# Reordering a load queue: a block's rows and first bias ahead of its second-layer weights in the mixed rounds of an expert stage

## The chip, the cores and the metric

One Trainium2 chip, one core, one program. The metric is the device time of one execution in microseconds (us); the time of a kernel is the median of its runs. The hardware profiler took one execution of the kernel before, and every row below comes from that execution. Its engines are TensorE (PE; PEld is its weight load), VectorE (DVE), ScalarE (ACT), GpSimd (POOL) and the queue of SyncE (SP), which issues nearly all loads.

## The reference

A one-layer vision transformer over 16 images of 256 tokens, width 256: patch embedding, gated decay attention, and a mixture of experts. The change lies in the last part, which computes

```python
logits = xf @ w_router
probs = jax.nn.softmax(logits, axis=-1)
topk_w, topk_idx = jax.lax.top_k(probs, TOP_K)
mask = jax.nn.one_hot(topk_idx, NUM_EXPERTS, dtype=xf.dtype)
weights = jnp.sum(topk_w[..., None] * mask, axis=1)
h = jnp.einsum('te,ieh->tih', xf, w1) + b1
h = jax.nn.gelu(h)
out = jnp.einsum('tih,ihe->tie', h, w2) + b2
out = jnp.sum(out * weights[..., None], axis=1)
```

with 4096 tokens, 8 experts, two experts to a token, width 256 and hidden width 1024, all in float32.

## The kernel before, in words

The engines run five hand-written instruction streams that meet through counting semaphores; no scheduler reorders them. Each stream is in order: an instruction that waits holds up all behind it on its engine.

The expert stage gathers the tokens of one expert into blocks. 31 blocks of 256 rows and 9 units of 128 rows are worked through in a fixed order, numbered by j. j = 0 to 21 are blocks (a first kind up to 3, then plain ones). From j = 22 on, blocks and units alternate: 9 rounds of one block and one unit, called the **mixed rounds**. A block splits its weights, rows and activations into a high and a low part and multiplies three times (L1494, L1506). A unit multiplies once in float32 straight from the loaded weights (L1519, L1530).

A block or unit j needs five loads: its rows from `expert_rows` (261 KB for a block, L402; half for a unit, L408), weights of layer 1 and 2 (1024 KB each, L388 and L392), the bias of layer 1 (4 KB, L396) and the bias of layer 2, spread to all partitions (128 KB, L399).

In one mixed round, call the block m, its unit u, and the next block n. TensorE's order is fixed: second half of layer 1 of m; transpose of u's rows (L1276); first half of layer 2 of m; first half of layer 1 of u (L1519); second half of layer 2 of m (L1506); transpose of n's rows (L1276, it waits for them to land); second half of layer 1 of u; half of layer 2 of u (L1530); first half of layer 1 of n; the rest of layer 2 of u.

The second half of layer 1 of u writes over four PSUM banks, so its first matmul waits until ScalarE has done the gelu of u's first chunk. That gelu (L887, into `q_s` or `k_s`; of the eight chunks of a block it goes into `mid_f`) waits for both biases of u on one semaphore:

```python
if c == 0:
    act.wait_ge(M[f"b_in{k.par}"], 32 * (k.n + 1))
```

The loads are issued by `load_pair(one, nxt, after, parity)`, once per round, eight times in all; there `one` is u, `nxt` is n and `after` is the block behind n. Its steps and the waits in them:

- `load_one(u)`: rows of u, w1 and b1 of u, then w2 of u when the unit before has finished its layer 2 (L570).
- `weights2_ahead(n)`: w2 of n, when VectorE has converted w2 of m (L556).
- `bias2(u)`: b2 of u, when the output of the unit before is taken (`y_done`).
- `rows_whole(n)`: rows of n, when VectorE has worked out the weights of m's rows (L531, `wsel_done`, set by L1918; m's rows lie in the same buffer), then b1 of n when ScalarE has done all gelus of m (L533, `gel_done`).
- `weights1_ahead(after)`: w1 of the block behind n (L550).
- `bias2(n)`: b2 of n, when m's output is taken (L1925).

Between the steps SP reads the expert's number and the list's place from a table (L411, L414). ScalarE converts w2 of n (L881) between the gelus of u, from the fifth on; VectorE follows with the low part (L1932). All these loads go through SP's one DMA queue; GpSimd issues the scattered additions to the output (L711).

Of the kernel before, what the change touches and what calls it, by code (L numbers as in the profile page):

```python
# [75 lines left out]
def vit_layer(nc, xT, w_tok, gamma, wq, wk, wv, wg, wa, ba, wo, gn_w, gn_b,  # L76
# [3 lines left out]
    with ExitStack() as ctx:  # L80
# [266 lines left out]
        def _(sp):  # L347
# [39 lines left out]
            def load_w1(e, staged, m):  # L387
                sp.dma_start(staged.rearrange("p (k n) -> p k n", k=EC),  # L388
                             w1[bass.ds(e, 1), :, :].rearrange("a (k p) n -> (a p) k n", p=P)).then_inc(M[m], 16)

            def load_w2(e, staged, m):
                sp.dma_start(staged.rearrange("p (k n) -> p k n", k=HC),  # L392
                             w2[bass.ds(e, 1), :, :].rearrange("a (k p) n -> (a p) k n", p=P)).then_inc(M[m], 16)

            def load_b1(e, par):
                sp.dma_start(b1_sb[par], b1[bass.ds(e, 1), :, :].rearrange("a p k -> (a p) k")).then_inc(M[f"b_in{par}"], 16)  # L396
# [4 lines left out]
            def load_rows(r, par):  # L401
                sp.dma_start(rows_f[par], lists_d[bass.ds(r, BLK), :].rearrange("(s p) n -> p s n", p=P)).then_inc(M[f"row_in{par}"], 16)  # L402
# [4 lines left out]
            def load_unit(r, par):  # L407
                sp.dma_start(rows_f[par][:, 0, :], lists_d[bass.ds(r, P), :]).then_inc(M[f"row_in{par}"], 16)  # L408

            def expert(j):  # L410
                return sp.value_load(tab[0:1, bass.ds(j, 1)], min_val=0, max_val=X - 1)  # L411

            def place(j):
                return sp.value_load(tab[0:1, bass.ds(j + NT, 1)], min_val=0, max_val=X * CAP)  # L414
# [110 lines left out]
            def rows_whole(k):  # L525

                e, r = expert(k.j), place(k.j)
                if isinstance(k.b, int) and k.b < 2:
                    sp.wait_ge(M["o_ps"], 2 * NP * NPR)
                sp.wait_ge(M["xe_ps"], EC * (k.j - 1))  # L530
                sp.wait_ge(M["wsel_done"], k.j - 1)  # L531
                load_rows(r, k.par)
                sp.wait_ge(M["gel_done"], HC * (k.j - 1))  # L533
                load_b1(e, k.par)

            def bias2(k):

                e = expert(k.j)
                sp.wait_ge(M["y_done"], YB * (k.j - 1))
                load_b2(e, k.par)  # L540
# [6 lines left out]
            def weights1_ahead(k, parity):  # L547

                e = expert(k.j)
                sp.wait_ge(M["w1_lo"], WQ * (k.b - 1))  # L550
                load_w1(e, w1_stage[parity], ("w1_in0", "w1_inx")[parity])

            def weights2_ahead(k):

                e = expert(k.j)
                sp.wait_ge(M["w2_lo"], WQ * k.b)  # L556
                load_w2(e, w2_f[0], "w2_in0")

            def load_one(k):

                e, r = expert(k.j), place(k.j)
                sp.wait_ge(M["wsel_done"], k.j - 1)
                load_unit(r, 1)
                sp.wait_ge(M["w1_lo"], WQ * NL)
                sp.wait_ge(M["hid_ps"], HC * (k.j - 1))
                load_w1(e, w1_f[1], "w1_in1")
                sp.wait_ge(M["gel_done"], HC * (k.j - 1))
                load_b1(e, 1)
                sp.wait_ge(M["w2_lo"], WQ * NL)
                sp.wait_ge(M["y_ps"], k.j - 1)  # L570
                load_w2(e, w2_f[1], "w2_in1")

            def load_pair(one, nxt, after, parity):

                load_one(one)
                weights2_ahead(nxt)
                bias2(one)
                rows_whole(nxt)
                if after is not None:
                    weights1_ahead(after, parity)  # L580
                bias2(nxt)
# [37 lines left out]
            def two_rounds(r):  # L619
                m0, u0, m1, u1 = four(r)  # L620
                load_pair(u0, m1, four(r + 1)[0], 0)
                load_pair(u1, four(r + 1)[0], four(r + 1)[2], 1)

            two_rounds(0)
            with sp.Fori(1, ROUNDS - 1) as r:
                two_rounds(r)
            m0, u0, m1, u1 = four(ROUNDS - 1)
            load_pair(u0, m1, four(ROUNDS)[0], 0)
            load_pair(u1, four(ROUNDS)[0], None, 0)
            load_one(four(ROUNDS)[1])  # L630
# [1591 lines left out]
```

## Time and profile before

| what | us |
|---|---|
| median of 3 runs (1324.74 to 1326.38) | 1326.38 |
| the profiled execution's own time | 1323.79 |
| its span, first to last instruction | 1321.9 |
| TensorE busy in the span | 1250.9 (95%) |
| ScalarE busy | 858.5 (65%) |
| VectorE busy | 825.2 (62%) |
| GpSimd busy | 428.1 (32%) |

The profiled execution's own time is 1.9 us over its span. The mixed rounds fill about 1120 to 1300 us of the span. In a row of a timeline the columns are start, duration, engine, line, operation, the tile written and the tile read, the shape and, in brackets, the idle time ahead of it with what ended it; consecutive instructions of one kind are merged into one row (x8). "SPq" is the queue of SyncE; an issue's duration is the time the queue spent on it, not the transfer's.

### The profile page before, as it was taken

How to read it: one execution, taken by the hardware profiler on the slowest of the kernel's cores; microseconds unless marked ns; L12 is line 12 of the kernel's file. 1: busy time of each engine (PE TensorE's matmuls, PEld its weight loads, DVE VectorE, ACT ScalarE, POOL GpSimd, SP SyncE). 2: the span in 40 equal slices, each digit the busy share in tenths (PEclk: the TensorE clock that was granted, in tenths of full speed). 3: DMA queues.
4: the chain of work that ended last, by engine and by line, in shares of the span. 5: the costliest groups of instructions: out<-in, count | busy, mean ns of one | idle time of the engine just before them, and what ended most of it. 6: DMA issues, size and time to landing. Idle time of an engine off the chain costs nothing. (4 is left out here: it accounts for less than half of the span.)

```text
span 1321.9 us, 27298 instructions
## 1 busy us (share of the span) xinstructions
PE 1250.9 (95%) x8534; PEld 1072.3 (81%) x8534; DVE 825.2 (62%) x2119; ACT 858.5 (65%) x2019; POOL 428.1 (32%) x524
## 2 busy tenths in 40 slices
PE   3899999999999999999999999999999999999996
PEld 2676777878778778778778778889999999989996
DVE  4455556665665665665665566657788888565552
ACT  2557577576576576576576565636788888666662
POOL 2021211241241241241141142164444544433434
PEclk7799999999999999999999999999999999999998
DMA  5321331341331331341332236458888787888873
GB/s 193 121 93 61 105 98 47 117 131 46 117 129 49 109 128 57 108 130 57 108 114 63 89 102 186 161 179 245 282 238 222 222 237 188 262 257 262 249 232 88
DMA packets 125607, 194.46 MB, mean 147 GB/s; under 512 B 16272, under 2 KB 91504, under 8 KB 125360
## 3 DMA queue, kind: packets, MB, share of 16 engines
q1 hardware_dynamic: 111920, 175.91, 41.5%
q0 software_dynamic: 13584, 17.26, 6.4%
q8 instruction: 54, 0.88, 0.3%
q14 instruction: 49, 0.40, 0.1%
HBM read 167.40 MB, written 29.05 MB: 149 GB/s over the span
## 5 line engine op out<-in xcount | busy, mean ns | idle before, releaser
L1161 PE MATMUL bank<-xn_sp,big_r 128*128 128x512 f32 x1152 | 312.1, 408 | 0.0
L1161 PEld LDWEIGHTS bank<-xn_sp,big_r 128*128 128x128 f32 x1152 | 204.6, 188 | 53.2 <-issue 1.4
L1674 DVE TENSOR_TENSOR att<-bank,dec_x 128x384 f32<-128x384 f32 x256 | 130.7, 552 | 110.1 <-PE bank L1198 108.9
L817 ACT ACTIVATE dec_x<-dec_x,ncum 128x256 f32<-128x256 f32 (+1 forms) x512 | 189.7, 444 | 5.7 <-POOL dec_x L654 5.7
L654 POOL TENSOR_SCALAR_AFFINE_SELECT dec_x<-dec_x 128x256 f32<-128x256 f32 x256 | 103.6, 434 | 215.8 <-DMA dec_x<-cum_scratch 215.7
L1494 PE MATMUL bank<-big_r 128*128 128x256 f32 x1296 | 168.0, 286 | 1.5 <-ACT mid_f L887 1.0
L1494 PEld LDWEIGHTS bank<-big_r 128*128 128x128 f32 x1296 | 160.5, 192 | 3.3 <-ACT mid_f L887 1.4
L705 POOL TENSOR_SCALAR mid_f<-mid_f,dec_x 128x256 f32<-128x256 f32 x71 | 76.9, 1087 | 187.0 <-DVE mid_f L1925 184.6
L711 POOL DMA_INDIRECT out<-mid_f,tok x71 | 118.6, 1671 | 53.0 <-POOL mid_f L705 22.0
L1941 DVE TENSOR_TENSOR big_r<-mid_f,big_r 128x256 fp32r<-128x256 f32 x216 | 91.4, 424 | 69.5 <-ACT big_r L907 69.3
L887 ACT ACTIVATE mid_f<-bank,h 128x256 f32<-128x256 f32 x216 | 101.2, 477 | 43.5 <-PE bank L1494 22.1
L789 ACT ACTIVATE tq<-bank 128x512 f32<-128x512 f32 x64 | 38.3, 598 | 140.3 <-PE bank L1161 140.3
L1932 DVE TENSOR_TENSOR big_r<-big_f,big_r 128x512 fp32r<-128x512 f32 x148 | 102.0, 695 | 7.1 <-ACT big_r L881 0.4
L1154 PE MATMUL bank<-big_r,xn_sp 128*128 128x512 f32 x384 | 97.7, 393 | 0.0
L1237 PEld LDWEIGHTS bank<-big_r,y_sp 128*128 128x128 f32 x768 | 95.5, 191 | 1.9
L1237 PE MATMUL bank<-big_r,y_sp 128*128 128x256 f32 x768 | 96.8, 284 | 0.0
L794 ACT ACTIVATE tq<-bank 128x512 f32<-128x512 f32 x64 | 38.2, 596 | 89.2 <-PE bank L1161 89.1
L1209 PE MATMUL bank<-att,mid_f 128*64 128x256 f32 x512 | 85.6, 407 | 10.4 <-ACT big_f L822 8.0
L1195 PE MATMUL bank<-q_s,k_s 64*128 64x256 f32 x512 | 91.0, 432 | 4.2 <-issue 4.2
L676 POOL DMA_INDIRECT expert_rows<-xn,slot x64 | 69.0, 1078 | 76.6 <-DVE slot L1809 60.4
L881 ACT ACTIVATE big_r<-big_f 128x512 fp32r<-128x512 f32 x148 | 93.5, 636 | 0.0
L907 ACT ACTIVATE big_r<-mid_f 128x256 fp32r<-128x256 f32 x216 | 91.7, 425 | 0.0
(217 smaller groups left out, 2231.4 us busy)
## 6 DMA issues: line engine op xcount, KB each, us to landing
big_f<-in_L_ffn_w SPq DMA_DIRECT2D x68, 1024.0 KB, 6.2
dec_x<-cum_scratch SPq DMA_DIRECT2D x128, 384.0 KB, 3.5
big_w<-in_L_ffn_w SPq DMA_DIRECT2D x12, 1024.0 KB, 6.7
mid_f<-expert_rows SPq DMA_DIRECT2D x27, 261.0 KB, 3.4
xt<-in_x SPq DMA_DIRECT2D x16, 256.0 KB, 3.7
h_scratch<-h SPq DMA_DIRECT2D x16, 256.0 KB, 2.3
h<-h_scratch SPq DMA_DIRECT2D x8, 512.0 KB, 4.3
out<-h SPq DMA_DIRECT2D x16, 256.0 KB, 4.0
```

Source lines behind the costliest of these rows:

```text
L654: pool.affine_select(out=d, in_=d, pattern=[[0, 2], [1, P]], compare_op=ALU.is_ge, fill=fill, base=0, channel_multiplier=-1).then_inc(M["c ...
L711: pool.indirect_dma_start(out=out_rows, out_offset=bass.IndirectOffsetOnAxis(ap=tok[k.par][:, s:s + 1], axis=0), in_=yo[k.par][:, s, :], i ...
L817: act.activation(d, d, ACT.Exp, bias=ncum[p % 2][:, NS * u + s, 2 * c + hh:2 * c + hh + 1]).then_inc(M["exp_done"], 1)
L881: act.activation(parts[0].rearrange("p k n -> p (k n)")[:, cols], staged[:, cols], ACT.Copy).then_inc(M[f"{name}_hi"], 1)
L887: act.activation(target, bank[hbank[c % HB]][:, 0:width], ACT.Gelu_apprx_tanh, bias=b1_sb[k.par][:, c:c + 1]).then_inc(M["gel_done"], 1)
L907: act.activation(g_sp[0][:, c, :], gel[c % NGEL], ACT.Copy).then_inc(M["gh_done"], 1)
L1154: mm = pe.matmul(bank[target][:, :], xp[:, k, t * P:(t + 1) * P], wp[:, k, n * 512:(n + 1) * 512], start=(k == 0 and j == 0), stop=(k == E ...
L1161: mm = pe.matmul(bank[target][:, :], wp[:, k, c * P:(c + 1) * P], xp[:, k, :], start=(k == 0 and j == 0), stop=(k == EC - 1 and j == 2))
L1237: mm = pe.matmul(bank[target][:, s * E:(s + 1) * E], yp[:, j, u * S + s * P:u * S + (s + 1) * P], wp[:, GC * g + j, :], start=(j == 0 and ...
L1494: mm = pe.matmul(bank[hbank[c % HB]][:, 0:BLK], wp[:, i, c * P:(c + 1) * P], xp[:, i, :], start=(i == 0 and j == 0), stop=(i == EC - 1 and ...
L1674: dve.tensor_tensor(att[hh][:, :], bank[4 + hh][:, 0:LW], dec[n % RING][:, hh, :], ALU.mult).then_inc(M["mult_done"], 1)
L1932: dve.tensor_tensor(lo, staged[:, cols], f32(hi), ALU.subtract).then_inc(M[f"{name}_lo"], 1)
```

## The change

Inside `load_pair`, `rows_whole(nxt)` moves from behind `bias2(one)` to a place ahead of `weights2_ahead(nxt)`. Nothing else differs.

```diff
             def load_pair(one, nxt, after, parity):
 
                 load_one(one)
+                rows_whole(nxt)
                 weights2_ahead(nxt)
                 bias2(one)
-                rows_whole(nxt)
                 if after is not None:
                     weights1_ahead(after, parity)
                 bias2(nxt)
```

The instructions of TensorE, VectorE, ScalarE and GpSimd stand in the same order as before. SP's differ in the eight rounds. The first `load_pair`, from the place where w2 of the unit has been issued, before (L392 is w2 of n, L399 b2 of u, L402 the rows of n):

```order
L392 ISA [waits w2_lo]
L392 DMA big_f<-in_L_ffn_w 128x8x256
L411 TENSOR_LOAD tab
L411 ISA x2
L399 ISA [waits y_done]
L399 DMA tq<-in_L_ffn_b 128x256
L411 TENSOR_LOAD tab
L411 ISA x2
L414 TENSOR_LOAD tab
L414 ISA x2
L402 ISA [waits wsel_done,xe_ps]
L402 DMA mid_f<-expert_rows 128x2x261
```

The same place on SP in the changed kernel, from the rows of n on:

```order
L402 ISA [waits wsel_done,xe_ps]
L402 DMA mid_f<-expert_rows 128x2x261
L396 ISA [waits gel_done]
L396 DMA h<-in_L_ffn_b 128x8
L411 TENSOR_LOAD tab
L411 ISA x2
L392 ISA [waits w2_lo]
L392 DMA big_f<-in_L_ffn_w 128x8x256
L411 TENSOR_LOAD tab
L411 ISA x2
L399 ISA [waits y_done]
L399 DMA tq<-in_L_ffn_b 128x256
```

The two waits of `rows_whole` (on `wsel_done` with `xe_ps`, and on `gel_done`), its two table reads and its two transfers now stand ahead of w2 of n and b2 of u. Right behind b2 of u, in the loop, the difference reads:

```order
 L399 ISA [waits y_done]
 L399 DMA tq<-in_L_ffn_b 128x256
-L411 TENSOR_LOAD tab
-L411 ISA x2
-L414 ISA
-L414 TENSOR_LOAD tab
-L414 ISA x2
-L530 REGISTER_ALU
-L402 ISA [waits wsel_done,xe_ps]
-L402 DMA mid_f<-expert_rows 128x2x261
-L533 REGISTER_ALU
-L396 ISA [waits gel_done]
```

There b2 of u is now followed at once by w1 of the block behind n.

## Rows read from the trace of the kernel before

**Rows 1.** Busy time by stretch: the mixed rounds (columns in the first row).
```profile
core 0: us, PE busy (x) PEld busy (x) DVE busy (x) ACT busy (x) POOL busy (x), PEclk, DMA share, GB/s
...
1120.00:1300.00 180.00, 171.75 (x1343) 166.85 (x1342) 103.92 (x273) 118.21 (x321) 73.75 (x56) 1.00 0.84 247
```

**Rows 2.** Groups by line, mixed rounds: busy us, mean ns | idle before, releaser.
```profile
L887 ACT ACTIVATE q_s<-bank,h 128x128 f32<-128x128 f32 x64 | 20.9, 366 | 22.6 <-DMA tq<-in_L_ffn_b 22.5
...
L1276 PE MATMUL bank<-ident,mid_f 128*128 128x128 f32 x54 | 9.2, 279 | 7.7 <-DMA mid_f<-expert_rows 7.6
```

**Rows 3.** SP's waits, mixed rounds: total us, times, longest.
```profile
SPq L531 <- DVE dec_x L1918: 9.9, 7, 2.0
```

**Rows 4.** Timeline of SP's queue, one mixed round.
```profile
1194.06 1.60 SPq L392 DMA_DIRECT2D big_f<-in_L_ffn_w  x2
1196.41 0.49 SPq L399 DMA_DIRECT2D tq<-in_L_ffn_b  x1
1200.45 0.37 SPq L402 DMA_DIRECT2D mid_f<-expert_rows  x1
1201.07 0.35 SPq L396 DMA_DIRECT2D h<-in_L_ffn_b  x1
1202.27 0.37 SPq L388 DMA_DIRECT2D big_w<-in_L_ffn_w  x1
1205.43 0.35 SPq L399 DMA_DIRECT2D h<-in_L_ffn_b  x1
```

**Rows 5.** Timeline of VectorE, same round.
```profile
1200.07 0.16 DVE L1918 TENSOR_TENSOR dec_x<-dec_x 128x2 f32<-128x2 f32 x1
```

**Rows 6.** Timeline of ScalarE, same round.
```profile
1199.87 0.47 ACT L887 ACTIVATE mid_f<-bank,h 128x256 f32<-128x256 f32 x1
...
1203.89 1.14 ACT L887 ACTIVATE q_s<-bank,h 128x128 f32<-128x128 f32 x4 [1.91 <-DMA tq<-in_L_ffn_b]
...
1206.09 0.62 ACT L881 ACTIVATE big_r<-big_f 128x512 fp32r<-128x512 f32 x1
...
1209.69 0.47 ACT L887 ACTIVATE mid_f<-bank,h 128x256 f32<-128x256 f32 x1 [0.66 <-PE bank L1494]
```

**Rows 7.** Timeline of TensorE, same round and the transpose of the next.
```profile
1204.68 0.65 PE L1276 MATMUL bank<-ident,mid_f 128*128 128x128 f32 x4
1205.17 1.95 PE L1519 MATMUL bank<-xs,big_f 128*128 128x128 f32 x16
...
1225.64 0.66 PE L1276 MATMUL bank<-ident,mid_f 128*128 128x128 f32 x4 [1.55 <-DMA mid_f<-expert_rows]
```

**Rows 8.** DMA issues at 1194.06 (w2 of u): KB, us to landing.
```profile
big_f<-in_L_ffn_w SPq DMA_DIRECT2D x1, 1024.0 KB, 5.7
```

**Rows 9.** Line L392 (w2), plain blocks, 940 to 1125 us.
```profile
DMA to landing us min/median/max: 8.3/8.8/10.2
```

**Rows 10.** Line L388 (w1), plain blocks, 940 to 1125 us.
```profile
DMA to landing us min/median/max: 5.3/5.9/7.4
```

**Rows 11.** Timeline of TensorE around 730 us (attention stage).
```profile
728.70 0.70 PE L1195 MATMUL bank<-q_s,k_s 64*128 64x256 f32 x4
...
732.83 0.75 PE L1209 MATMUL bank<-att,mid_f 128*64 128x256 f32 x4 [3.21 <-ACT big_f L822]
...
733.93 1.23 PE L1195 MATMUL bank<-q_s,k_s 64*128 64x256 f32 x4
```

**Rows 12.** Busy time by stretch (columns as in rows 1), attention stage.
```profile
733.30:736.70 3.40, 3.40 (x17) 2.43 (x14) 2.54 (x4) 0.42 (x1) 0.76 (x2) 0.50 0.94 285
```

**Rows 13.** Busy time by stretch (columns as in rows 1), a mixed round.
```profile
1162.00:1166.00 4.00, 1.43 (x13) 1.23 (x12) 1.52 (x6) 1.45 (x6) 1.82 (x2) 1.00 0.87 315
```

**Rows 14.** Timeline of TensorE in that stretch.
```profile
1165.13 0.66 PE L1276 MATMUL bank<-ident,mid_f 128*128 128x128 f32 x4 [2.57 <-DMA mid_f<-expert_rows]
```

**Rows 15.** DMA issues, plain blocks, 900 to 1100 us: KB, us to landing.
```profile
mid_f<-expert_rows SPq DMA_DIRECT2D x16, 261.0 KB, 2.9
```

**Rows 16.** The page's part 6, whole span: KB, us to landing.
```profile
h_scratch<-h SPq DMA_DIRECT2D x16, 256.0 KB, 2.3
```

## The prediction

> **What bounds the kernel now.** I began with the busy time by stretch. In the mixed rounds, the only place the change touches, TensorE is busy 171.75 of 180 us at full clock [rows 1]: TensorE sets the pace, and a change is worth what it does to TensorE's 8.25 idle us or to new idle time. The groups by line say what that idle time is: 7.6 us of it stand ahead of the transpose of the next block's rows, waiting for those rows to land [rows 2]. The same view shows a second late load that costs TensorE little yet: the first gelu of the unit waits 22.5 us in all, eight times, for b2 of the unit, the bias load that the change moves back [rows 2].
>
> Next I asked what holds the rows back. SP waits in `rows_whole` seven times, 9.9 us in all, for VectorE's L1918 [rows 3]. The timelines of one round show it: L1918 runs from 1200.07 to 1200.23 [rows 5], the rows are issued at 1200.45 [rows 4]. SP was free long before: b2 of u had gone at 1196.41. So in seven rounds of eight the rows are not held by what stands ahead of them in the queue; they are held by VectorE, and that stays.
>
> **The change, part by part.** I take the issue of n's rows as time 0 of a round (1200.45 here), since by the last paragraph it does not move.
>
> *The rows.* Issued no earlier, they still land sooner, because 2048 KB of w2 and 128 KB of b2 are no longer just ahead of them. With little ahead, the same transfer lands after 2.9 us [rows 15]. TensorE wants them 4.2 us after the issue (1204.68 in a round without a wait [rows 7]). So the wait for the rows goes: **minus 7.6 us**. More than 7.6 cannot come from this.
>
> *w2 of n.* Before, it follows w2 of u within the same merged row, at 1194 to 1196 [rows 4]. Now it stands behind the rows and behind b1, whose wait is for m's last gelu; that gelu ends at 1199.87 + 0.47 = 1200.34, ahead of the rows' own release, so b1 stays at +0.62 (1201.07). The next issue in the queue came at +1.82 (1202.27, then w1) after one table read; w2 of n now takes that slot, with one table read as well.
>
> *b2 of u.* It comes behind w2 of n: 0.37 us for the issue, then 0.75 for the table read (the pair of w2 ends at 1194.06 + 1.60 = 1195.66, b2 starts at 1196.41 [rows 4]): +2.94, where it used to be at -4.04. This is the price of the change, because the unit's first gelu needs it.
>
> When does it land? No row shows w2 alone behind rows alone. The nearest is w2 of u, issued at 1194.06 with little ahead of it: 5.7 us to landing [rows 8]. The lower bound is the fastest 1024 KB transfer of the plain blocks, 5.3, the upper the slowest, 7.4 [rows 10]. I take 5.7, which has the same size, shape and stage: w2 of n lands at +7.52. b2's 128 KB come behind it in the same queue: in the plain blocks w2 follows w1 by about half a us and lands 2.9 us later by the medians (8.8 [rows 9] against 5.9 [rows 10]), so 1024 KB more cost some 3.4 us and 128 KB an eighth of it, 0.43. b2 lands at +7.95. The row before agrees with such a queue: b2 went out at 1196.41 behind 2048 KB, and the gelu that waited for it began at 1203.89, 7.5 us later [rows 4, 6].
>
> By the Trainium skill ("DMA: Bandwidth & Descriptors", section "Anatomy of one DMA — SWDGE (gpsimd) path") a transfer takes about 2.0 us plus its bytes at 436 GB/s; as an estimate that is 4.4 us for w2 and 0.3 more for b2, and the sum below would be 9.8 instead of 21.2 us. The trace disagrees: no 1024 KB load of this stage's neighbour came under 5.3 [rows 10], so the rows go into the sum.
>
> *What waits for b2.* ScalarE's first gelu of u takes 0.37 us [rows 2] and ends at +8.32. TensorE's second half of layer 1 of u (L1519) needs its bank; without any wait it begins at 1205.17, +4.72 [rows 7]. TensorE is thus idle from +4.72 to +8.32: **3.6 us**, with bounds 3.2 and 5.3. Nothing else can fill it, as TensorE's order is fixed. Eight rounds: 8 x 3.6 = **plus 28.8 us**.
>
> *What is hidden.* w2 of n itself: ScalarE wants it 2.2 us after the unit's first gelu (1206.09 against 1203.89 [rows 6]), that is at +10.15, and it lands at +7.52; 2.6 us of cover, lost only if w2 takes over 8.3 us. w1 of the block behind n is issued some 2 us later and is used a round later: nothing. b2 of n comes behind that w1: +7.95 + 3.4 + 0.4 = +11.8, and the block's first gelu wants it 5.8 us after the unit's (1209.69 against 1203.89 [rows 6]), at +13.75: hidden by 1.9 us; without that cover each us late costs up to 8 us in all.
>
> *The clock.* TensorE's idle stretch would be longer than any in the mixed rounds now. In the attention stage an idle stretch of 3.21 us [rows 11] was followed by 3.4 us at clock 0.50 [rows 12], the 1.2 GHz level; one of 2.57 us in the mixed rounds [rows 14] kept 1.00, 2.4 GHz [rows 13]. Four matmuls of L1195 took 0.70 us at the full level and 1.23 at the lower [rows 11], so 3.4 us at half cost about 3.4 x (1 - 0.70 / 1.23) = 1.5 us. The stalls of 3.6 us lie just over the one that was followed by a fall; I take a fall in half of the eight rounds: **plus 6 us**, bounds 0 and 12.
>
> *Sum.* -7.6 + 28.8 = +21.2, and 6 for the clock: 27 us on the profiled execution's 1323.8 gives 1351. That execution lies 2.6 us below the median of the runs and 1 below the lowest; I add 1 and predict **1352 us**. Moves within 0.2% (2.7 us) are about what a measurement of this kernel cannot tell from no change.
>
> **The rivals.**
>
> *R1, the clock falls in every round.* All of the above, but eight falls: 1323.8 + 21.2 + 12 = 1357. For it: 3.21 us of idle sufficed once. Against: one case, in a stage whose matmuls are of other shapes. The Trainium skill ("TensorE: Matmul & The Clock Gate", section "Why this matters for your kernels") advises against idle gaps of about this length between bursts of matmuls, since one such gap brings the lower level back; by that rule all eight fall. Rows 11 and 12 agree with it, and no run here has yet shown it for these matmuls.
>
> *R2, b2 does not queue behind w2.* If small transfers slip past a large one, b2 lands 2.3 [rows 16] to 2.9 us [rows 15] after its issue: +5.2 to +5.85, a stall of 0.9 to 1.5 us, in sum -0.4 to +4.4: 1323 to 1328, no change to slightly slower. Against: b2 took 7.5 us before.
>
> *R3, faster.* The wait for the rows goes and b2 comes in time. It decides at b2's landing: with a stall under 0.95 us (7.6 / 8), so a landing under 2.3 us from issue, the change pays; at +4.35, 1.4 us from issue, it pays in full: 1316. Against: the shortest landing of the page's loads and stores is that 2.3 [rows 16], with little else in flight.
>
> *R4, the other loads come late too.* If w2 takes the 7.4 us of rows 10, the stall is 5.3 us, and b2 of n lands near its need as well: 8 x 5.3 - 7.6 = +34.8, with the falls up to 1370.
>
> *That the change does not do what it says* is half true in all cases: the rows go first in the queue, but not earlier.
>
> **How the numbers follow.** Forecast 0.73, R1 0.10, R4 0.06, R2 0.08, R3 0.03. Half of R2 lies within 0.2%. Slower: 0.73 + 0.10 + 0.06 + 0.04 = 0.93; the same 0.04; faster 0.03. For the range: the forecast without falls and with the 5.3 us landing gives 8 x 3.2 - 7.6 = +18, 1342; R2 and R3 below it are left out but for a margin toward them, and the end of R4 above; 1338 to 1367.
>
> **What would show it.** In the changed profile the rows of n should still go out some 0.4 us after L1918 starts; b1, w2, b2 and w1 should follow at +0.6, +1.8, +2.9 and about +4. TensorE's wait for the rows should be gone; ScalarE's wait for b2 should grow from 22.5 us to about 22.5 + 8 x 4.4 (b2 lands at +7.95 instead of +3.44) less what the rounds shift; TensorE should be idle about 3.6 us ahead of L1519, eight times, and the clock row should dip there in some rounds. I am wrong if b2 lands within 3 us of its issue, if L1918 is not what the rows wait for, or if TensorE's idle time in the mixed rounds does not grow.

## The result, and the profile after

The change makes the kernel slower: 1370.93 us median (1369.71 to 1372.46, 4 runs) against 1325.56 us (1324.7 to 1326.38, 4 runs), a ratio of 1.0343 with a 95% interval of 1.0325 to 1.0361, or 45 us. The sign and the mechanism are those of the prediction. The size is not: 27 us were forecast, and 1371 lies above the range.

Busy time of the mixed rounds, by stretch (columns as in rows 1), kernel after:

```profile
1120.00:1346.00 226.00, 189.70 (x1351) 183.33 (x1350) 106.13 (x269) 120.56 (x324) 70.59 (x56) 0.90 0.69 195
```

The stretch is 46 us longer than that of rows 1, as the stage takes some 45 us more. TensorE is now idle in it for 36 us instead of 8, and it is also busy for 18 us longer with the same work, at a mean clock of 0.90 where rows 1 had 1.00. Two losses, then, of unlike kind. The waits of the same stretch (us in total, times, longest us) name the first:

```profile
ACT q_s L887 <- DMA tq<-in_L_ffn_b: 58.4, 8, 8.5
...
PE bank L1519 <- ACT q_s L887: 36.2, 8, 5.4
...
PEld bank L1276 <- DMA mid_f<-expert_rows: 0.3, 1, 0.3
```

ScalarE waits for b2 of the unit (tq is its place) for 58.4 us instead of 22.5 [rows 2]. TensorE, which lost 7.6 us to the rows [rows 2], no longer waits for them, but waits 36.2 us ahead of L1519 for the unit's first gelu. The wait of SP that stands ahead of the rows grew:

```profile
SPq L531 <- DVE dec_x L1918: 35.3, 8, 4.7
```

against 9.9 us before [rows 3]: SP now arrives there earlier and stands longer, in front of w2 and b2. One round on SP's queue (L402 rows of the next block, L396 b1, L392 w2, L399 b2, L388 w1):

```profile
1219.54 0.38 SPq L402 DMA_DIRECT2D mid_f<-expert_rows  x1
1220.17 0.35 SPq L396 DMA_DIRECT2D h<-in_L_ffn_b  x1
1221.35 0.37 SPq L392 DMA_DIRECT2D big_f<-in_L_ffn_w  x1
1222.48 0.35 SPq L399 DMA_DIRECT2D tq<-in_L_ffn_b  x1
1223.66 0.37 SPq L388 DMA_DIRECT2D big_w<-in_L_ffn_w  x1
```

VectorE, ScalarE and TensorE in the same round, one fence each:

```profile
1219.16 0.16 DVE L1918 TENSOR_TENSOR dec_x<-dec_x 128x2 f32<-128x2 f32 x1
```

```profile
1228.58 1.14 ACT L887 ACTIVATE q_s<-bank,h 128x128 f32<-128x128 f32 x4 [7.51 <-DMA tq<-in_L_ffn_b]
```

```profile
1223.47 0.60 PE L1276 MATMUL bank<-ident,mid_f 128*128 128x128 f32 x4
1229.01 3.78 PE L1519 MATMUL bank<-xs,big_f 128*128 128x128 f32 x16 [4.94 <-ACT q_s L887]
1232.58 2.40 PE L1530 MATMUL bank<-big_f,q_s 128*128 128x256 f32 x8
```

The rows go out 0.38 us after L1918 begins, exactly as before (1200.07 and 1200.45 [rows 5, 4]): first in the queue, yet not a moment earlier. b2 follows at +2.94 and its gelu begins at +9.04. TensorE has the next block's rows transposed by 1224.07 and then stands for 4.94 us. When it resumes, 16 matmuls of L1519 take 3.78 us instead of 1.95 [rows 7]: the second loss. Over all rounds the mean of one L1519 instruction is 345 ns:

```profile
L1519 PE MATMUL bank<-xs,big_f 128*128 128x128 f32 x272 | 47.0, 345 | 36.2 <-ACT q_s L887 36.2
```

It was 275 ns in the kernel before. The clock in the round shown, by stretch:

```profile
1219.50:1229.00 9.50, 4.57 (x40) 4.33 (x38) 4.07 (x12) 1.99 (x6) 3.48 (x3) 0.88 0.70 223
1229.00:1233.50 4.50, 4.50 (x19) 4.32 (x20) 2.75 (x5) 4.50 (x13) 1.56 (x1) 0.50 0.82 203
```

The fall begins before TensorE resumes and is still there 4.5 us later. How much work runs at the lower level differs from round to round. The longest and the shortest such stretch, each from the moment TensorE resumes:

```profile
1255.10:1260.90 5.80, 5.80 (x22) 5.35 (x23) 3.52 (x6) 4.70 (x13) 2.00 (x2) 0.50 0.76 167
1281.90:1284.80 2.90, 2.90 (x13) 2.90 (x14) 1.45 (x3) 2.90 (x9) 1.86 (x2) 0.50 1.02 259
```

All eight stalls have such a stretch behind them; together they make 34 us.

### The profile page after: what moved, and what is told of

It is laid out like the page before. It is cut to its first block and busy times, and to the rows that moved or that the text cites. A ratio compares the mean times of both kernels' runs of the same rounds, so it can differ in the third digit from the quotient of the medians.

```text
span 1370.5 us, 27298 instructions
## 1 busy us (share of the span) xinstructions
PE 1269.9 (93%) x8534; PEld 1089.1 (79%) x8534; DVE 826.1 (60%) x2119; ACT 859.8 (63%) x2019; POOL 426.5 (31%) x524
## 5 line engine op out<-in xcount | busy, mean ns | idle before, releaser
L887 ACT ACTIVATE mid_f<-bank,h 128x256 f32<-128x256 f32 x216 | 101.2, 477 | 52.2 <-PE bank L1494 30.5
L711 POOL DMA_INDIRECT out<-mid_f,tok x71 | 115.4, 1625 | 48.6 <-POOL mid_f L705 24.5
L1209 PE MATMUL bank<-att,mid_f 128*64 128x256 f32 x512 | 85.5, 406 | 10.3 <-ACT big_f L822 8.0
L881 ACT ACTIVATE big_r<-big_f 128x512 fp32r<-128x512 f32 x148 | 93.4, 635 | 0.0
```

Source lines behind the costliest of these rows:

```text
L711: pool.indirect_dma_start(out=out_rows, out_offset=bass.IndirectOffsetOnAxis(ap=tok[k.par][:, s:s + 1], axis=0), in_=yo[k.par][:, s, :], i ...
L881: act.activation(parts[0].rearrange("p k n -> p (k n)")[:, cols], staged[:, cols], ACT.Copy).then_inc(M[f"{name}_hi"], 1)
L887: act.activation(target, bank[hbank[c % HB]][:, 0:width], ACT.Gelu_apprx_tanh, bias=b1_sb[k.par][:, c:c + 1]).then_inc(M["gel_done"], 1)
```

## The experiments

My theory after this result: b2 of the unit, queued behind w2 of the next block, costs TensorE about 29 us net, and the half-clock stretches that the stalls bring (clock 0.50, the 1.2 GHz level) cost the rest, some 16 to 19. Rivals: w2 itself comes too late; the late issue hurts whatever is ahead; the long matmuls come from contention, not from the clock.

The profiled executions also differ ahead of the mixed rounds, where nothing was changed: w2 of the first unit goes out at 1130.74 us in the profile of before, and between 1132.78 and 1136.96 in the others. So beside the medians I compare, in the profiled executions, the time from that issue (the first L392 of the mixed rounds) to the end of the span. It is 191.2 us before and 236.2 after: plus 45.0. Each ratio in the table is to executions of before from the same series, with medians of 1325.56 us for the changed kernel, 1325.62 for e1 to e4 and 1324.63 for e5 to e7.

| kernel | median us | ratio to before, 95% interval | us from that issue to the end |
|---|---|---|---|
| before | 1325.56 | | 191.2 |
| after | 1370.93 | 1.0343 (1.0325 to 1.0361) | 236.2 |
| e1_b2_first | 1319.74 | 0.9941 (0.9927 to 0.9955) | 183.1 |
| e2_b2_before_w2 | 1331.81 | 1.0043 (1.0026 to 1.0061) | 196.3 |
| e3_filler | 1375.2 | 1.0355 (1.0334 to 1.0375) | 239.9 |
| e4_w1_last | 1363.85 | 1.0272 (1.0253 to 1.0291) | 230.3 |
| e5_filler16 | 1358.1 | 1.0252 (1.0224 to 1.028) | 220.7 |
| e6_split | 1366.23 | 1.032 (1.0291 to 1.0349) | 230.0 |
| e7_b2_first_rows_last | 1328.88 | 1.0032 (1.0015 to 1.0048) | 194.9 |

### e1_b2_first: is it b2, or w2?

```diff
                 load_one(one)
+                bias2(one)
                 rows_whole(nxt)
                 weights2_ahead(nxt)
-                bias2(one)
```

> The changed kernel, but b2 of the unit goes out right behind w2 of the unit, ahead of the rows of the next block; w2 of the next block stays behind the rows. Theory (the loss comes from b2 queued behind w2 of the next block, not from w2 being late): b2 is there when ScalarE wants it, the rows land about 3 us after their issue, TensorE waits neither for rows nor ahead of L1519; the clock stays at 1.00 in the mixed rounds; ScalarE waits some 1.7 us per round for w2 ahead of its first L881, under TensorE's work. Time about 1318 us, 7 to 8 below the kernel before. Rival (w2 of the next block, now issued 6 us later, is itself the cause): ScalarE's wait for w2 holds up the later gelus, TensorE waits 2 to 4 us per round, time 1340 to 1360 us.

Measured: 1319.74 us, 0.6% faster than before and the fastest kernel of the study; a gain of 6 us where 7 to 8 were expected. One round on SP, with b2 ahead of the rows:

```profile
1193.49 0.33 SPq L399 DMA_DIRECT2D tq<-in_L_ffn_b  x1
1198.38 0.38 SPq L402 DMA_DIRECT2D mid_f<-expert_rows  x1
1199.01 0.33 SPq L396 DMA_DIRECT2D h<-in_L_ffn_b  x1
1200.18 0.38 SPq L392 DMA_DIRECT2D big_f<-in_L_ffn_w  x1
```

w2 of the next block goes out 1.80 us after the rows, as late as in the changed kernel (1.81). ScalarE does wait for it, about 2 us a round (waits of the mixed rounds):

```profile
ACT y_sp L881 <- DMA big_f<-in_L_ffn_w: 8.1, 4, 2.7
ACT big_r L881 <- DMA big_f<-in_L_ffn_w: 7.9, 4, 2.5
```

But TensorE has other work then (by stretch):

```profile
1120.00:1296.00 176.00, 175.19 (x1378) 171.21 (x1377) 105.54 (x276) 119.57 (x330) 75.98 (x56) 1.00 0.86 253
```

It is busy for 175.19 of 176 us, at full clock. So a late w2 costs nothing here; the whole loss hangs on b2. ScalarE's wait also shows when w2 lands: its first L881 begins 5.4 to 5.8 us after w2's issue in seven of the eight rounds and 7.2 in the first. The rows are waited for no more than 0.4 us in all:

```profile
L1276 PE MATMUL bank<-ident,mid_f 128*128 128x128 f32 x54 | 8.9, 273 | 0.4 <-DMA mid_f<-expert_rows 0.4
```

### e2_b2_before_w2: the queue, or the moment of the issue?

```diff
                 rows_whole(nxt)
-                weights2_ahead(nxt)
                 bias2(one)
+                weights2_ahead(nxt)
```

> The changed kernel with b2 of the unit and w2 of the next block swapped: b2 is still issued behind the rows and both of their waits, 1.8 us after the rows instead of 2.9, but no 1024 KB transfer is ahead of it. Theory (the queue behind w2 is what costs): b2 lands about 3 us after its issue, the unit's first gelu starts 4.7 to 5.0 us after the rows' issue, TensorE waits 0.3 to 0.8 us per round, time 1320 to 1327 us. Rival (the late issue costs, whatever is ahead): b2 lands 5 to 6 us after its issue, TensorE waits 2.5 to 3.5 us per round, time 1338 to 1350 us.

Measured: 1331.81 us, 5 us over the theory's range and well under the rival's. One round, SP and then ScalarE:

```profile
1184.83 0.38 SPq L402 DMA_DIRECT2D mid_f<-expert_rows  x1
1185.48 1.05 SPq L396 DMA_DIRECT2D h<-in_L_ffn_b  x1
1187.28 0.34 SPq L399 DMA_DIRECT2D tq<-in_L_ffn_b  x1
```

```profile
1190.43 1.14 ACT L887 ACTIVATE q_s<-bank,h 128x128 f32<-128x128 f32 x4 [4.07 <-DMA tq<-in_L_ffn_b]
```

With no large transfer ahead b2 lands 3.2 us after its issue; with w2 ahead it took 6.1 (1222.48 to 1228.58). That is the queue. What remains is the moment: b2 is still issued behind the rows (at +2.45 here, at +1.7 to +2.0 in the other rounds), late enough for TensorE to wait 9.3 us in all:

```profile
L1519 PE MATMUL bank<-xs,big_f 128*128 128x128 f32 x288 | 37.1, 284 | 9.3 <-ACT q_s L887 9.3
```

So both count. The edit moves both at once, but the rounds keep them apart: in the mean of eight, the unit's first gelu begins 3.4 us earlier than in the changed kernel (+5.4 against +8.8); 1.1 of that is the earlier issue, 2.3 the shorter time from issue to landing. The queue is about two thirds. The time is over the theory's range, and the record accounts for that only in part: 9.3 - 7.6 is 1.7 of the 5.1 us between 191.2 and 196.3, and the stall of the first round, 3.14 us where the others are 0.5 to 1.3, brought a half-clock stretch of 3.4 us.

### e3_filler and e5_filler16: the clock, or contention?

Both keep TensorE busy while it waits for b2, between the transpose of the rows and L1519; e5 has 16 in the place of 32.

```diff
                 turn_rows(nxt, rows_f[0], BS)
+                for _ in range(32):
+                    pe.matmul(bank[7][:, 0:P], ident[:, :], ident[:, :], start=True, stop=True)
                 one1(k, two)
```

> The changed kernel with 32 matmuls of the identity into an unused PSUM bank ahead of the second half of layer 1 of the unit, in the time in which TensorE waits for b2; they add work that the reference does not have and feed nothing. Theory (TensorE's idle stretch lets the clock fall, and the fall costs some 19 of the 45 us): no half-clock stretch in the mixed rounds, L1519 takes 1.95 us per 16 again, b2 lands as late as before; time 1350 to 1356 us. Rival (L1519 and L1530 take longer because the loads and ScalarE's copies run beside them): the longer matmuls stay, time 1368 to 1378 us.

Measured: 1375.2 us, a miss of the number, and from this time alone the rival looked right. The groups of the mixed rounds say otherwise:

```profile
L1559 PE MATMUL bank<-ident 128*128 128x128 f32 x512 | 58.5, 275 | 0.0
...
L1519 PE MATMUL bank<-xs,big_f 128*128 128x128 f32 x256 | 31.2, 275 | 0.0
```

The filler (L1559) took 58.5 us, 7.3 a round, so it covered the stall and ran on past it. L1519 itself is back at the 275 ns of before (it was 345 in the changed kernel). TensorE is busy for 224.71 of 226 us at clock 1.00. So the part of the theory on the clock holds, and the rival's longer matmuls did not stay; the time went to the filler. e5 has half of it:

> As e3_filler, with 16 filler matmuls instead of 32: the 32 took 7.3 us per round, more than the stall of 4.5 us; 16 should take 3.65. They add work that the reference does not have and feed nothing. Theory (the half-clock stretches cost some 16 us, the stalls some 29): the clock stays at 1.00 in the mixed rounds, L1519 takes 1.95 us per 16, TensorE's remaining wait is 0.7 to 1.0 us per round, time 1352 to 1357 us. Rival (without the falls TensorE only waits longer for the same loads): the rounds keep their length, time 1368 to 1373 us.

Measured: 1358.1 us, 13 less than the changed kernel, though TensorE does more work; 1 us above the theory's range, 10 below the rival's. Groups and busy time of the mixed rounds of e5:

```profile
L1519 PE MATMUL bank<-xs,big_f 128*128 128x128 f32 x288 | 35.9, 278 | 8.2 <-ACT q_s L887 8.2
...
L1559 PE MATMUL bank<-ident 128*128 128x128 f32 x256 | 29.9, 275 | 0.0
```

```profile
1120.00:1336.00 216.00, 207.27 (x1653) 202.38 (x1652) 109.19 (x281) 122.42 (x335) 72.82 (x57) 1.00 0.73 209
```

Filler and remaining wait make 38.1 us, about the 36.2 us of stall of the changed kernel; the clock stays at 1.00; from the first w2 to the end it takes 220.7 instead of 236.2 us. So the clock is worth 15.5 us, or 17 if the 2 us of longer waiting are taken off; by the medians alone it would be 13. The loads and copies that would have made the contention are all still there, and L1519 takes 278 ns and not 345: contention is out.

### e4_w1_last: why b2 landed later than I had worked out

```diff
                 bias2(one)
+                bias2(nxt)
                 if after is not None:
                     weights1_ahead(after, parity)
-                bias2(nxt)
```

> The changed kernel with w1 of the block after next issued behind b2 of the next block, so that nothing follows b2 of the unit in the queue for some 2 us. Theory (w1, issued 1.2 us behind b2, takes a share of the DMA engines and delays b2's landing by about 1 us): b2 lands 4.8 to 5.0 us after its issue as in the last round of the changed kernel, TensorE waits 3.3 to 3.6 us per round, time 1358 to 1364 us. Rival (the landing is set by what is ahead of b2): 5.9 us as before, time 1369 to 1373 us.

Measured: 1363.85 us, at the upper end of the theory's range. One round on SP, and the unit's first gelu:

```profile
1198.70 0.35 SPq L399 DMA_DIRECT2D tq<-in_L_ffn_b  x1
1200.93 0.34 SPq L399 DMA_DIRECT2D h<-in_L_ffn_b  x1
1202.24 0.38 SPq L388 DMA_DIRECT2D big_f<-in_L_ffn_w  x1
```

```profile
1203.65 1.14 ACT L887 ACTIVATE q_s<-bank,h 128x128 f32<-128x128 f32 x4 [6.39 <-DMA tq<-in_L_ffn_b]
```

b2 lands 4.95 us after its issue. In the second to the seventh round it is 4.6 to 5.3 us here, 5.0 in the mean, and 5.4 to 6.2 in the changed kernel, 5.9 in the mean. In the last round no w1 follows in either kernel, and they agree (4.9 and 4.8). So the load that follows 1.2 us behind b2 delays it by about 1 us. TensorE's wait falls from 36.2 us to 31.0:

```profile
PE bank L1519 <- ACT q_s L887: 31.0, 8, 6.0
```

That is 3.9 a round, over the 3.3 to 3.6 expected, because of the first round alone: there b2 takes 7.0 us with nothing behind it (6.8 in the changed kernel), and TensorE waits 6.0. Why the first round is slow stays open; w1 is not the reason. The other seven wait 3.3 to 3.9.

### e6_split: a us of issue for a us of stall

`rows_whole` is taken apart: the rows ahead, b1 with its wait behind b2 of the unit.

```diff
                 load_one(one)
-                rows_whole(nxt)
+                rows_alone(nxt)
                 weights2_ahead(nxt)
                 bias2(one)
+                bias1_alone(nxt)
```

> The changed kernel with only the rows moved ahead: b1 of the next block, with its wait for the last gelu, goes behind b2 of the unit. So w2 and b2 are issued about 1.2 us earlier. Theory (each us by which b2 goes out later is a us of TensorE's stall): the stall falls by 1.0 to 1.2 us per round from 4.5, time 1357 to 1363 us. Rival (the landing is set by the DMA engines' load, not by the issue): 1369 to 1373 us.

Measured: 1366.23 us, between the two ranges. One round on SP, and TensorE's wait (L1533 is this kernel's number for L1519, L901 for L887):

```profile
1192.38 0.38 SPq L402 DMA_DIRECT2D mid_f<-expert_rows  x1
1193.71 0.37 SPq L392 DMA_DIRECT2D big_f<-in_L_ffn_w  x1
1194.85 0.34 SPq L399 DMA_DIRECT2D tq<-in_L_ffn_b  x1
1196.00 0.34 SPq L396 DMA_DIRECT2D h<-in_L_ffn_b  x1
1197.34 0.38 SPq L388 DMA_DIRECT2D big_f<-in_L_ffn_w  x1
```

```profile
PE bank L1533 <- ACT q_s L901: 29.3, 8, 4.3
```

The edit was worth less than I had thought: b2 went out 2.47 us after the rows instead of 2.94, half a us and not 1.2. TensorE's wait fell from 36.2 to 29.3 us, 0.9 a round, more than half a us of issue explains. The rows show what else changed: w1 now follows 2.5 us behind b2 instead of 1.2, with only the 4 KB of b1 between. That fits e4, where a later w1 let b2 land sooner, but no run separates the two.

### e7_b2_first_rows_last: where the gain of e1 comes from

```diff
                 load_one(one)
-                rows_whole(nxt)
-                weights2_ahead(nxt)
                 bias2(one)
+                weights2_ahead(nxt)
+                rows_whole(nxt)
```

> The kernel before with b2 of the unit ahead of w2 of the next block, the rows where they were, last. It asks where the gain of e1_b2_first comes from. Theory (from the rows, which land sooner when w2 of the next block is not ahead of them): ScalarE's wait for b2 goes, TensorE still waits 6 to 9 us in all for the rows, time 1324 to 1327 us. Rival (from b2 being early): TensorE's wait for the rows is of no weight without the wait for b2, time 1317 to 1321 us.

Measured: 1328.88 us, 0.3% slower than before, 2 us over the theory's range and 8 over the rival's. ScalarE's waits for b2 all but vanish, yet TensorE waits for the rows even longer than the theory had it (waits of the mixed rounds):

```profile
PE bank L1276 <- DMA mid_f<-expert_rows: 10.3, 8, 3.5
```

The longest of these waits, 3.5 us, brought a half-clock stretch. e7 and e1 differ only in the place of `rows_whole`, behind w2 of the next block or ahead of it; that place takes TensorE's wait for the rows from 10.3 us to 0.4 and the time from the first w2 to the end from 194.9 to 183.1 us. So e1's gain lies in the rows having no w2 ahead of them, as the change intended; b2 must go out before both.

## Why the prediction was wrong in size

**The rows (right).** Forecast minus 7.6 us; the wait of 7.6 is 0.3 in the changed profile, on the weight load alone. As forecast, it is L1918 that releases them and not the queue, now in all eight rounds.

**The order of issues (right).** b1, w2 and b2 were put at +0.62, +1.82 and +2.94; the round shown has +0.63, +1.81 and +2.94.

**b2's landing (too early by 0.9 us a round, the first step that failed).** It stands under "What is hidden": w1 of the block behind was put at nothing because its own use is a round away; what it does to b2, 1.2 us ahead of it in the queue, was not weighed. The unit's first gelu began at +8.8 in the mean of the eight rounds (+9.04 in the round shown), not at +7.95, and TensorE stood 36.2 / 8 = 4.5 us, not 3.6: 7.4 us more in all. e4 takes w1 away from there and with it 5.2 of the 7.4; the other 2.2 are the slow first round, whose cause is open. The landing of w2 itself, put at 5.7, is 5.4 to 5.8 in seven rounds of e1; in the changed kernel nothing waits for it, so it cannot be read there.

The Trainium skill's rule for a transfer ("DMA: Bandwidth & Descriptors", section "Anatomy of one DMA — SWDGE (gpsimd) path"), a fit for transfers that GpSimd issues, gave, as an estimate, 4.7 us from w2's issue to b2's landing. The trace has 7.2 for these loads of SP (1221.35 to 1228.58), and 6.1 in e4 without w1 behind them (1197.57 to 1203.65), so measurement and rule differ here.

**The clock (too small by 10 us, the second step that failed).** I took a fall in half of the rounds at 1.5 us each, 6 us, with 12 as the bound. All eight stalls brought one. And each cost more: I had priced 3.4 us of work at the lower level, from a single fall in another stage; here it was 2.9 to 5.8 us after TensorE had resumed, 34 in all. (The mean clock of 0.90 over 226 us gives some 45 us at 1.2 GHz; the rest of these lie inside the stalls, where they cost nothing.) At the rate of L1519's 16 matmuls, 34 x (1 - 1.95 / 3.78) is 16.4 us. What 45.0 leaves over the net stall (36.2 - 7.6 = 28.6) is 16.4 too, and e5 gives 15.5 to 17. Rival R1 was right that every stall would have its fall, as the Trainium skill's page "TensorE: Matmul & The Clock Gate" (section "Why this matters for your kernels") has it for gaps of that length; eight of eight agree. R1's price was too low as well.

**Hidden terms (right).** w2 of the next block stayed hidden from TensorE: e1 issues it just as late and TensorE is idle for 0.8 us in 176. In the changed kernel ScalarE does not wait for it at all.

Together: -7.6, plus 36.2 in place of 28.8, plus 16.4 in place of 6, is 45.0 us instead of 27. Either miss alone would have stayed inside the range (1359 or 1362); both together did not. The range itself was too narrow for its own terms: the upper bounds of the stall and of the clock, with the 1 us added, make 1371, and 1367 left that end out.

**By luck.** R4's 1370 lies next to the measured 1371, but by another way: it wanted w2 to take 7.4 us and every stall to be 5.3, where w2 took 5.4 to 5.8 in seven rounds of e1 and the mean stall was 4.5; the falls of the clock, dearer than R4 had them, made up the rest. The forecast for ScalarE's wait, 22.5 + 8 x 4.4 (by its own figures 4.5), is 57.7, and 58.4 was measured; two errors cancel in it. Before, the gelu began at +4.3 in the mean of eight rounds, and not at the +3.44 of the one round read; after, at +8.8 and not at +7.95.

R2 and R3 fell: b2 does queue behind w2 (6.1 us against 3.2 without it).

## What to carry to other kernels

Before a load is moved ahead in a queue, ask what releases it: here the rows' own wait held them, so putting them first issued them no earlier and put their wait in front of every load behind them. And look at what follows closely behind a load in its queue, not only at what is ahead of it. Find the load whose consumer has the least slack, however small it is, and issue it ahead of both the wait and the large transfers; with b2 there, the same move of the rows gains 0.6% instead of losing 3.4%. And price a new TensorE stall of the lengths seen here with the half-clock work behind it: some 2 us a stall, on top of the stall itself.

## What the runs showed of the hardware

- Stalls of 3.3 to 5.4 us of TensorE were each followed by work at 1.2 GHz, in eight of eight rounds, for 2.9 to 5.8 us; so were the single stalls of 3.14 us in e2 and 3.5 us in e7, while the 2.57 us of rows 14 were not. In the round shown the lower level was there before TensorE resumed and for 4.5 us of dense matmuls after. 16 matmuls took 3.78 us instead of 1.95. Matmuls that compute nothing of use, placed in the wait, kept the clock at 1.00 and saved 13 us in the median.
- A 1024 KB load issued 1.2 us behind one of 128 KB in the same queue delayed the earlier one's landing by about 1 us (5.9 against 5.0 us in the mean of six rounds); in the first round it made no difference.
- A float32 matmul of 128 x 128 with 128 columns stands in the trace as two instructions: the 32 fillers of a round are 64 rows, 512 in eight rounds, and take 7.3 us.
